# Causal and non-causal attention on one core: four heads' value products per burst, bans and bias moved off TensorE

## The reference, cut to what matters

```python
qkv = layernorm(t) @ w_qkv                       # (4, 256, 3*256)
s = q @ k.T * 16 ** -0.5                         # per image and head, 256 x 256
if causal: s = where(key <= query, s, -inf)      # the second attention only
t = t + (softmax(s) @ v) @ w_proj + b_proj
```

## Time and profile before

| what | value |
|---|---|
| median of 3 runs | 1068.17 us (1067.59 to 1070.4) |
| the profiled execution | 1069.0 us, span 1067.2 us |
| PE busy | 877.1 us (82%) |
| DVE busy | 452.5 us (42%) |
| ACT busy | 295.6 us (28%) |
| POOL busy | 204.1 us (19%) |
| mean granted PE clock | 0.883 of full speed |
| "a2": from the first unit to its last residual add | 315.35 to 410.46 us |
| "a3": from the first unit to its last residual add | 647.66 to about 745.7 us |

### The profile page before, as it was taken

How to read it: one execution, slowest core, us unless ns; L and a number is a source line. 1 busy time by engine, 2 the same in 40 slices (tenths; PEclk the granted TensorE clock), 3 DMA queues, 4 the chain that set the end, 5 groups by cost and what they waited for, 6 DMA issues and landing times. The chain is left out here.

```text
span 1067.2 us, 12919 instructions
## 1 busy us (share of the span) xinstructions
PE 877.1 (82%) x4252; PEld 555.6 (52%) x4253; DVE 452.5 (42%) x937; ACT 295.6 (28%) x446; POOL 204.1 (19%) x280
## 2 busy tenths in 40 slices
PE   4678389898768996399999378998379999999994
PEld 2666246336434554166565245665346666666662
DVE  4973522897546433522222555551622122122122
ACT  3223336431324351021221133333112222222221
POOL 1240000770001000233343101000111211211210
PEclk7589579999869996599999689998579999999997
DMA  3000060000347202032111334850202205710103
GB/s 105 1 1 1 19 228 1 0 1 1 88 117 193 66 1 87 15 106 96 49 41 38 129 95 145 208 149 1 87 20 68 100 20 189 312 40 20 29 15 128
DMA packets 53771, 80.26 MB, mean 75 GB/s; under 512 B 10297, under 2 KB 46141, under 8 KB 50525
## 3 DMA queue, kind: packets, MB, share of 16 engines
q1 hardware_dynamic: 48192, 67.25, 20.1%
q0 software_dynamic: 5536, 12.46, 3.8%
HBM read 55.69 MB, written 11.27 MB: 63 GB/s over the span
## 5 line engine op out<-in xcount | busy, mean ns | idle before, releaser
L1996 PE MATMUL psum<-ring,f_x_t 128*128 x552 | 253.8, 603 | 1.3 <-DVE f_x_t L1864 1.3
L1857 DVE TENSOR_TENSOR f_gated<-f_silu,psum 128x512 f32<-128x512 f32 x69 | 47.4, 687 | 270.4 <-PE psum L1996 270.4
L1996 PEld LDWEIGHTS psum<-ring,f_x_t 128*128 128x128 f32 x552 | 101.4, 194 | 104.3 <-issue 104.2
L2010 PE MATMUL psum<-ring,f_gated_t 128*128 x552 | 130.7, 380 | 1.8 <-ACT f_gated_t L1923 1.8
L2010 PEld LDWEIGHTS psum<-ring,f_gated_t 128*128 128x128 f32 x552 | 101.2, 190 | 23.5 <-issue 12.8
L1282 DVE TENSOR_REDUCE a_maxima<-psum 128x2 f32<-128x512 f32 x128 | 82.9, 687 | 61.5 <-PE psum L1440 32.2
L1923 ACT ACTIVATE f_gated_t<-psum 128x512 f32<-128x512 f32 x69 | 41.2, 597 | 236.6 <-PE psum L2003 236.6
L1919 ACT ACTIVATE f_silu<-psum 128x512 f32<-128x512 f32 x69 | 41.2, 597 | 113.6 <-PE psum L1996 113.6
L1374 ACT ACTIVATE a_expo<-psum 128x1024 f32<-128x1024 f32 (+1 forms) x64 | 58.3, 911 | 40.6 <-PE psum L1471 24.5
L1437 PE MATMUL psum<-a_stack_k,a_stack_q 96*128 96x256 bf16 (+1 forms) x256 | 49.7, 277 | 20.9 <-DMA a_stack_k<-a_parts 11.8
L1489 PE MATMUL psum<-a_expo,a_values 128*32 128x256 f32 (+1 forms) x512 | 61.3, 358 | 0.0
(11 more groups left out here) (294 smaller groups left out, 1232.0 us busy)
## 6 DMA issues: line engine op xcount, KB each, us to landing
ring<-in_f_experts SPq DMA_DIRECT2D x24, 1536.0 KB, 7.7
a_stack_q<-a_parts SPq DMA_DIRECT2D x96, 64.0 KB, 2.9
a_stack_k<-a_parts SPq DMA_DIRECT2D x96, 64.0 KB, 2.9
rows_in<-h SPq DMA_DIRECT2D x4, 1024.0 KB, 6.8
ring<-rows_out SPq DMA_DIRECT2D x8, 512.0 KB, 5.4
a_wqkv<-in_a_wqkv SPq DMA_DIRECT2D x2, 768.0 KB
x_in<-in_x SPq DMA_DIRECT2D x1, 1024.0 KB, 4.9
out<-x SPq DMA_DIRECT2D x4, 256.0 KB, 2.1
```

Source lines behind the costliest of these rows:

```text
L1857: dve.tensor_tensor(gated[:, b, :], silu[:, b, :], psum[:, 2 * b + 1, :], ALU.mult).then_inc(s_g, 1)
L1996: last = pe.matmul(psum[:, 2 * b + side, :], x_t[:, xb, t, :], k.ring[:, bass.ds(at + start, CHUNK)], start=(t == 0), stop=(t == CT - 1))
L2010: last = pe.matmul(psum[:, Y_BANK, 0:C], gated_t[:, b, P * a:P * a + P], k.ring[:, bass.ds(at + start, C)], start=(c == 0 and a == 0), sto ...
```

## The change

1. `weigh_values` takes a quad (four heads, two units) at a time instead of a unit: it is called after `scores_less_max` of every even unit i, for quad i/2 - 1, and for the last quad at the end. The loop goes over key tiles outside and the four heads (column tiles) inside. The exponentials get twice the buffers (the second two lie in k.h, which is free there).
2. In the causal attention the ban matmuls go. For the maxima, VectorE adds a float32 table `later` to the PSUM scores and reduces with max in one instruction, one over 128 keys and one over 256 for each head, in place of one reduction over 512 elements. For the exponentials, GpSimd sets the entries above the diagonal to zero with affine_select after the exponential: 128 partitions x 512 float32 for each unit. `weigh_values` waits for GpSimd instead of ScalarE.
3. The bias matmuls go. GpSimd adds b_proj (now 128 x 256) to the whole of k.t (128 x 2048) once, after the LayerNorm has been read.
4. Three small constants are no longer loaded by SP (ones, identity, bans); "a3" loads `later` (128 KB), and b_proj is 128 KB instead of 1 KB.

```diff
-        expo = sb("expo", [P, 2, 2, BANK])
+        expo_low = sb("expo", [P, 2, 2, BANK])
+        expo_high = k.h[:].rearrange("p t b n -> p (t b n)").rearrange("p (u j n) -> p u j n", u=2, j=2)
...
+        WEIGHTS = 4 if causal else 3
+        QUADS = GROUP // 4
+
+        def exponentials(i):
+            return (expo_low, expo_high)[i // 2 % 2][:, i % 2]
+
...
             pool.memset(values[:, :, :, HD:], 1.0).then_inc(s_ones, 1)
-
-            for g in range(GROUPS):
+            pool.wait_ge(s_ones, 1)
+            pool.wait_ge(s_w, 16 * WEIGHTS)
+            pool.wait_ge(ln.s_out, TT)
+            pool.tensor_tensor(k.t[:], k.t[:], b_proj[:].unsqueeze(1).broadcast_to([P, TT, C]), ALU.add).then_inc(s_bias, 1)
+
+            def load_max_rows(g):
                 pool.wait_ge(s_nl, g + 1)
                 pool.wait_ge(s_nh, g + 1)
                 for q in range(MAXROWS):
                     pool.dma_start(stack_q[STACK + q:STACK + q + 1, g % SLOTS_G], negated[:, g % SLOTS_G, q, :]
                                    ).then_inc(s_mr[g % 2], 16)
+
+            def zero_future(i):
+                pool.wait_ge(s_ex, i + 1)
+                on_diagonal = exponentials(i).rearrange("p j (m n) -> p j m n", m=NT)[:, :, :, 0:P]
+                pool.affine_select(on_diagonal, on_diagonal, [[0, 2], [0, NT], [1, P]], ALU.is_ge, 0.0, base=0,
+                                   channel_multiplier=-1).then_inc(s_sel, 1)
+
+            if causal:
+                load_max_rows(0)
+                for i in range(UNITS * GROUPS):
+                    zero_future(i)
+                    if maxima_complete(i + 1):
+                        load_max_rows(maxima_complete(i + 1))
+            else:
+                for g in range(GROUPS):
+                    load_max_rows(g)
...
                 dve.wait_ge(s_sc, i + 1)
+                if causal:
+                    for t in range(NT):
+                        keys = P * t + P
+                        last = dve.tensor_tensor_reduce(masked[:, i % 2, t, 0:keys], psum[:, i % 2, N * t:N * t + keys],
+                                                        later[:, N - keys:], 1.0, -3e38, ALU.add, ALU.max,
+                                                        maxima[:, g, t, h:h + 1])
+                    last.then_inc(s_mx, 1)
+                    return
                 dve.tensor_reduce(maxima[:, g, :, h], psum[:, i % 2, :].rearrange("p (t m) -> p t m", t=NT),
                                   AX_X, ALU.max).then_inc(s_mx, 1)
...
-                act.wait_ge(s_av, UNITS * (g + 1))
+                act.wait_ge(s_av, QUADS * (g + 1))
...
-                    if i >= 2:
-                        act.wait_ge(s_av, i - 1)
-                    act.activation(expo[:, i % 2, :, 0:WIDTH], psum[:, 2 + 2 * (i % 2):4 + 2 * (i % 2), 0:WIDTH],
+                    if i >= 4:
+                        act.wait_ge(s_av, i // 2 - 1)
+                    act.activation(exponentials(i)[:, :, 0:WIDTH], psum[:, 2 + 2 * (i % 2):4 + 2 * (i % 2), 0:WIDTH],
                                    ACT.Exp, scale=HD ** -0.5).then_inc(s_ex, 1)
...
-                                     stack_k[0:STACK, slot, h, 0:keys], start=True, stop=not causal)
-                    if causal:
-                        last = pe.matmul(psum[:, i % 2, N * t + P * t:N * t + P * t + P], ident16[:], bans[:, 0, :],
-                                         start=False, stop=True)
-                        if t == 0:
-                            pe.matmul(psum[:, i % 2, P:N], ident16[:], bans[:, 2, :], start=True, stop=True)
+                                     stack_k[0:STACK, slot, h, 0:keys], start=True, stop=True)
...
-                                         start=True, stop=not causal)
-                        if causal:
-                            last = pe.matmul(psum[:, bank, col:col + P], ident16[:], bans[:, 1, :], start=False, stop=True)
+                                         start=True, stop=True)
                 last.then_inc(s_s2, 1)
 
-            def weigh_values(i):
-                g, unit = i // UNITS, i % UNITS
+            def weigh_values(quad):
+                g = quad // QUADS
                 b, half = image_and_half(g)
-                pe.wait_ge(s_ex, i + 1)
-                if unit == 0 and g >= 2:
+                pe.wait_ge(s_sel, 2 * quad + 2)
+                if quad % QUADS == 0 and g >= 2:
 
                     pe.wait_ge(s_cn, g - 1)
                     image, projected = image_and_half(g - 2)
                     if projected:
                         pe.wait_ge(s_res, image + 1)
-                for j in range(2):
-                    h = 2 * unit + j
-                    q, col = 32 * (h % 4), N * (h // 4)
-                    for m in range(NT):
-                        first = n1 if m else 0
-                        last = pe.matmul(psum[q:q + 32, 6 + g % 2, col + first:col + N],
-                                         values[:, NT * b + m, GROUP * half + h, :], expo[:, i % 2, j, N * m:N * m + N - first],
+                col = N * (quad % QUADS)
+                for m in range(NT):
+                    first = n1 if m else 0
+                    for lane in range(4):
+                        h = 4 * (quad % QUADS) + lane
+                        last = pe.matmul(psum[32 * lane:32 * lane + 32, 6 + g % 2, col + first:col + N],
+                                         values[:, NT * b + m, GROUP * half + h, :],
+                                         exponentials(2 * quad + lane // 2)[:, lane % 2, N * m:N * m + N - first],
                                          start=(m == 0), stop=(m == NT - 1))
...
-                        pe.matmul(out, ctxn[:, b % 2, t, P * a:P * a + P], w_proj[:, t, :], start=(t == 0), stop=False)
-                    last = pe.matmul(out, ones[:], b_proj[:], start=False, stop=True)
+                        last = pe.matmul(out, ctxn[:, b % 2, t, P * a:P * a + P], w_proj[:, t, :], start=(t == 0), stop=(t == CT - 1))
...
-                    if i:
-                        weigh_values(i - 1)
+                    if i and i % 2 == 0:
+                        weigh_values(i // 2 - 1)
```

More of the change, by code:

```diff
@@ L1157, in attention @@
         w_proj = sb("w_proj", [P, CT, C])
-        b_proj = sb("b_proj", [1, C])
-        ones = sb("ones_row", [1, P])
-        ident16 = sb("ident16", [P, P], BF16)
-        bans = sb("bans", [P, 3, P], BF16)
+        b_proj = sb("b_proj", [P, C])
+        if causal:
+            later = sb("later", [P, N])
+            masked = sb("masked", [P, 2, NT, N], BF16)
         h_t = k.x1[:].rearrange("p t b n -> p t (b n)")
@@ L1200, in attention @@
         s_ex = sm("exponentials")
+        s_sel = sm("future_zeroed") if causal else s_ex
+        s_bias = sm("bias_added")
         s_av = sm("values_weighted")
@@ L1217, in _ @@
         def _(sp):
-            for dst, src in ((wqkv, w["wqkv"]), (w_proj, w["w_proj"]), (b_proj, w["b_proj"]), (ones, k.dram["ones"]),
-                             (ident16, k.dram["ident16"]), (bans, k.dram["bans"])):
+            for dst, src in ((wqkv, w["wqkv"]), (w_proj, w["w_proj"]), (b_proj, w["b_proj"])):
                 sp.dma_start(dst[:], src).then_inc(s_w, 16)
+            if causal:
+                sp.dma_start(later[:], k.dram["later"]).then_inc(s_w, 16)
             sp.dma_start(stack_k[STACK:].rearrange("r s h n -> r (s h n)"), k.dram["ones16"]).then_inc(s_ones_rows, 16)
@@ L1301, in add_residual @@
                 b, _ = image_and_half(g)
+                dve.wait_ge(s_bias, 1)
                 dve.wait_ge(s_pj, b + 1)
@@ L1304, in add_residual @@
                 dve.tensor_tensor(tile, tile, psum[:, 6 + g % 2, :], ALU.add).then_inc(s_res, 1)
+            if causal:
+                dve.wait_ge(s_w, 16 * WEIGHTS)
             for i in range(FIRST_MAXIMA):
@@ L1391, in _ @@
                 last.then_inc(s_ht, 1)
-            pe.wait_ge(s_w, 16 * 6)
+            pe.wait_ge(s_w, 16 * WEIGHTS)
             for i in range(2 * CT):
@@ L1544, in _ @@
                         scores_for_max(ahead)
-            weigh_values(UNITS * GROUPS - 1)
+            weigh_values(QUADS * GROUPS - 1)
             turn_contexts(GROUPS - 1)
@@ L2114, in _host_arrays @@
     a["iota"] = np.tile(np.arange(HW, dtype=np.float32), (P, 1))
-    a["ones"] = np.ones((1, P), np.float32)
     l1 = {n[8:]: m for n, m in f.items() if n.startswith("L1_conv_")}
@@ L2134, in _host_arrays @@
     above = np.where(order[None, :] > order[:, None], forbid, 0.0)
-    a["bans"] = np.stack([above, above.T, np.full((P, P), forbid)], 1).astype(bf16)
-    a["ident16"] = np.eye(P).astype(bf16)
+    a["later"] = np.concatenate([np.zeros((P, P)), above], 1).astype(np.float32)
     def dims_outermost(m):
@@ L2144, in _host_arrays @@
     a["a2_w_proj"] = tiles(f["L2_attn_w_proj"])
-    a["a2_b_proj"] = f["L2_attn_b_proj"].reshape(1, C)
+    a["a2_b_proj"] = np.tile(f["L2_attn_b_proj"].reshape(1, C), (P, 1))
```

(2 more changed lines are left out.)

## The result

The changed kernel takes 1029.66 us (median of 4 runs, 1028.62 to 1030.84), the kernel before in the same comparison 1067.88 us (1066.76 to 1070.4). The profiled execution took 1029.4 us, its span 1027.6.

What follows compares the result with a forecast made beforehand. PE was taken to bound both attentions until chains through ScalarE, GpSimd, VectorE and SP's queue take over. Savings of 14.6 us in a2 and 12.4 in a3, 27 off the span, gave 1041 us, range 1030 to 1059.

Steps and rivals of the forecast that it cites:

- the select's price: GpSimd's select in "a3", on the chain between bursts: 1.27 us a unit, taken from the two-input 512-element row.
- the forecast's own chain: In "a3", burst, heads, start of ScalarE, exponential and select add up to 3.94 us from burst to burst.
- groups 6 and 7 of "a3": Groups without maxima: 2 x 7.8 = 15.6 us against 15.85, 0.3 less, the select costing what the bans gave.
- The lower bound: Select in "a3" at 0.45 to 0.5 us, from below the memset's rate.
- the plain group of "a3": Group without projection: 2 x 3.94 + turn_back 0.3 + 0.6 = 8.9 us against 10.4, 1.5 less.
- the clock's terms in "a3": Before the first unit, a low clock costs 0.9 us net; at the end, bias removal gives 1.4 less.
- Group 0 of "a3": First group of "a3", with three maxima in a unit, 13.66 us before: 1.8 us less.
- The rival of two strips at a time: Four-head bursts overlap only two strips at a time, so an "a2" pair takes 4.05 us; 1058 in all, chance 0.10.
- Groups 1 and 2: Plain groups held by SP's queue of stack DMAs, 20.8 us at least: 0.2 less in "a2", 1.5 in "a3".
- The bias: Bias matmuls removed: each projection falls from 3.4 to 2.1 us, and each stage's end gives 1.4 less.
- The rival on the other side: Waits drop PE's clock to half: 1105 us in both attentions (chance 0.07), about 1067 in "a3" alone (0.04).
- Better than 1032: Whole kernel: a time below the forecast's own range of 1032 to 1050 us, chance 0.07.

Runs made afterwards that it cites:

- e4: The changed kernel with GpSimd's select done twice in every unit, so a unit costs GpSimd 1.28 us; 1038.42 us.
- e16: The changed kernel itself, nothing altered, measured again in another comparison on another chip; 1032.89 us.
- e2: The kernel before with only the bans moved to VectorE and GpSimd, bursts of two heads and the bias matmul kept; 1065.8 us.
- e6: The changed kernel with a burst's two loops swapped, heads outside and key tiles inside; 1028.68 us.
- e7: The changed kernel with the chunks of expert weights issued at groups 0, 5 and 6, none at groups 1 to 4; 1027.15 us.
- e13: The changed kernel with each value burst, and the turning and projection work, issued one unit later; 1036.17 us.
- e5: The changed kernel with SP issuing a group's stack DMAs ahead of its chunk of expert weights; 1025.67 us.
- e14: The changed kernel with bursts one unit later and a group's stack DMAs ahead of its chunk; 1035.24 us.

## Why the prediction was wrong, and where it was right

**The step that failed: the select's price, the largest single term.** I took 1.27 us, the two-input row of the same size, between 0.45 and 2.7. It is 0.64. With that one figure changed, the forecast's own chain gives 0.78 + 0.33 + 0.55 + 0.81 + 0.1 + 0.64 + 0.1 = 3.31 us from burst to burst, and 4 x 3.31 = 13.2 for groups 6 and 7 of "a3"; 13.31 was measured. In the forecast's sum this price stands four times in groups 6 and 7, twice in group 5 and once in each group with a projection (4.6 is 3.94 + 0.6), 8 x 0.63 = 5.0 us: 1036 instead of 1041. That is under half of the 11.3 us by which the whole misses the forecast, and the measured surplus of groups 3 to 7 is 4.0. e4 puts the price that I took back. It costs 8.4 us by the distances to before, 6.0 against e16 (4.3 by the ratios), but more than half of that in its profile comes from groups 6 and 7, where GpSimd's queue and the half clock add 4 us to what the forecast has at the same price. So e4 shows that the price matters on the chain, and not that it explains the miss alone. The lower bound that I had given covered 0.64, but its worth was under-sized: "about 3 us lower" for 0.77. The Trainium skill (GPSIMD Engine Reference, Performance versus the Vector engine) has 1.8 cycles an element at best, from which I had estimated 0.77 us; the trace's 0.64 is below it, and nearer to it than to my row. Slips of the sum changed little: 4 x 3.94 is 15.8 and not 15.6, the plain group of "a3" adds up to 8.8 and not 8.9, and 320 x 0.06 is 19 and not 18.

**The second: the clock's terms in "a3".** I charged 0.9 us for a low clock ahead of the first unit. The stretch from stage start to first unit fell by 2.8 instead (2.6 in e16, 1.7 in e2 with the bans alone). Its mean clock is 0.79 where before had 0.81, so the clock took nothing back and the removed bans, 2.0 us by the forecast, counted. At the end I had 1.4 us and got 2.9: before, the last 4.7 us ran at half clock, after they did not. That part is luck of one execution: e16 has 0.82 at its end, which takes 9.36 us instead of 7.75, and gains 1.3. These two terms make 5.2 us of the 10.9 by which "a3" gave more than forecast.

**Group 0 of "a3"** gave 3.6 us where I took 1.8. Here VectorE sets the time, and a head costs it 0.56 us from start to start (its two reductions, 0.29 and 0.42 us, overlap) where I took 0.62: 0.7 us for the twelve heads of that group. The rest may be the clock: after has 0.92 there, e16 0.65, and in e16 the group gave 1.9 us, as forecast.

**What turned into waits.** I had said that more than half of the PE work that goes turns into waits. By busy time it was about a third: from the first unit of "a3" to its last burst, PE was busy 82.6 of 88.4 us before and 55.8 of 70.8 after, 26.8 less work for 17.7 less time, and over the whole kernel 877.1 and 823.8 us, 53.3 less work for 38.2 less time.

**Right.** Four strips overlap: sixteen instructions in 1.07 us in "a2" and 0.86 in "a3", as eight did. The rival of two strips at a time is out, and by e6 the order inside the burst doesn't matter. Groups 1 and 2 took 18.4 and 19.5 us where the forecast had 19.7 and 19.4. That transfers hold them is shown by e7: without chunks there they took 17.0 and 16.1 us with the same stacks in SP's queue, so the chunks on the rings count beside the queue that I had named. The bias is 12.6 us alone and 12.2 in the whole. The add on GpSimd takes 4.5 us and nobody waits for it.

**The rival on the other side** was half there. No loop ran at the low clock all through, but in group 0 and after two waits of 1.8 us "a3" does for some microseconds (mean 0.90 from the first unit to the last burst, 1.00 before), e4 and e13 more. Two of the gaps ahead of it were not those which I had counted: the maxima rows' DMA, 5.6 us to landing behind stacks and chunks, was missing in the forecast. I had put the two DMAs on GpSimd's queue and not on the rings. The Trainium skill (TensorE: Matmul & The Clock Gate, Part 1) has half rate as the default that activity releases. The stretches behind a hole agree, with the clock at 0.50. But group 0 of e2 ran at 0.50 with PE busy 13.7 of 15.5 us, as the earlier trace rows had it with 3.5 of 4; what kept the clock down there was not found.

**The range.** It ended 0.34 us above the median of after; e16, the same kernel in another comparison, lies inside. "Better than 1032" had 0.07, and the select at its lower bound should have carried it further down. That the miss is so narrow is chance: the two medians of the same kernel, after and e16, lie 3 us apart.

**A version that may beat both** is e5, two lines of SP's order: 1025.67 us, ratio 0.9592 (0.9556 to 0.9628) to before. Its interval still touches that of after (0.9615 to 0.9658).

## What to carry to other kernels

Where an operation that the trace doesn't have lies on the chain between bursts, its price counts once for each burst that waits for it. Carry both bounds through that sum, with the clock after the longer wait, before the range is set. When matmuls are merged or moved, ask what hole they filled: in e13 the hole of 1.0 us that was left was followed by half clock. Count a small DMA that a chain needs as late as the transfers on the rings make it: here two rows of 4 KB landed behind 1.5 MB chunks, and TensorE waited up to 3.2 us for them (e7).

## What the runs showed of the hardware that I had not expected

- GpSimd's affine_select of 128 x 512 float32 took 0.64 us, half of its two-input operation of that size (1.27).
- VectorE's fused add and maximum from PSUM took 419 ns for 256 columns and 287 for 128. The trace shows an accumulator read of 83 ns behind each, which starts with the next one, so a head's two cost 0.56 us from start to start.
- GpSimd's DMAs of 4 KB (1.03 us to issue two) took 1.6 to 7.6 us to land, 5.6 at the median of 14, in a stretch of which two groups carried 243 GB/s.
- A single hole of 1.0 us behind the turning of the maxima (e13, e14) was followed by half clock, where the same stretch with the burst in the hole stayed at 1.00 (after, e16).
